# Batch 0's x and half its context loaded into rooms of their own, x's layernorm first, key stacks of the first group issued by ScalarE, and new orders

## The reference

```
h  = layernorm(x)                       # over the last axis, no weights
Q  = h @ Wq.T + bq;  K = ctx @ Wk.T + bk;  V = ctx @ Wv.T + bv
attention with 16 heads of 32, softmax over the 512 keys
x  = x + tanh(g_xattn) * (attention @ Wo.T + bo)
h  = layernorm(x)
e  = argmax(h @ router_w + router_b) of 8 experts, gate = its softmax value
x  = x + tanh(g_ffn) * gate * (h @ expert_w[e] + expert_b[e])
```

## Time and profile before

| | us |
|---|---|
| median of 3 runs | 1055.9 (1054.35 to 1056.93) |
| the profiled execution | 1057.68 |
| its span | 1056.0 |
| TensorE busy | 978.0 |
| ScalarE busy | 811.9 |
| VectorE busy | 745.6 |
| GpSimd busy | 262.0 |

### The profile page before, as it was taken

The page is one execution under the profiler, slowest core; times in us unless marked ns, Lnnn a source line. Parts: engine busy times, 40 slices in busy tenths (PEclk is TensorE's granted clock), DMA queues, the critical chain, the costliest instruction groups (busy, mean ns, idle before and its releaser), DMA issues.

```text
span 1056.0 us, 18686 instructions
## 1 busy us (share of the span) xinstructions
PE 978.0 (93%) x5208; PEld 641.8 (61%) x5208; DVE 745.6 (71%) x1653; ACT 811.9 (77%) x1913; POOL 262.0 (25%) x318
## 2 busy tenths in 40 slices
PE   3798999999999999999999999999999997698996
PEld 2564467656765676567656765676567545576775
DVE  5745655875787578757875787578757778797664
ACT  3688988898889888978898889888988988233431
POOL 6002200430042004200420042004201006454663
PEclk9799999999999999999999999999999989799999
DMA  6334223532443245324532453244325259144542
GB/s 213 97 90 114 79 64 98 143 85 69 115 137 89 69 110 140 89 60 117 136 81 70 117 137 84 68 116 137 86 69 132 62 166 378 56 135 137 163 138 75
DMA packets 70884, 119.37 MB, mean 113 GB/s; under 512 B 17854, under 2 KB 18878, under 8 KB 70656
## 3 DMA queue, kind: packets, MB, share of 16 engines
q1 hardware_dynamic: 64544, 99.49, 34.0%
q0 software_dynamic: 6240, 18.68, 5.5%
HBM read 50.42 MB, written 18.66 MB: 65 GB/s over the span
## 4 chain that ended last, share of the span: by engine, by line
PE 69%; ACT 10%; DVE 7%; issue 6%; DMA 3%; POOL 2%; SPq 2%; DVEq 1%; ACTq 0%; POOLq 0%
PE jb L489 11%; PE jb L490 10%; PE jb L491 10%; PE jb L532 10%; PE sc L512 9%; PE hb L522 9%; PE sc L673 6%; ACT jb L707 5%; ACT probs L695 3%; DVE maxima L819 1%; DVE e_lo L836 1%; PE hb L659 1%; PE jb L603 1%; SPq L452 1%; DMA q_stack<-q_lo 1%
## 5 line engine op out<-in xcount | busy, mean ns | idle before, releaser
L819 DVE TENSOR_REDUCE maxima<-jb 128x1 f32<-128x512 f32 x512 | 335.7, 686 | 112.0 <-PE jb L532 109.5
L707 ACT ACTIVATE jb<-jb,maxima 128x512 f32<-128x512 f32 x512 | 341.9, 678 | 41.4 <-DVE maxima L819 38.0
L695 ACT ACTIVATE probs<-sc 128x512 f32<-128x512 f32 x512 | 284.4, 605 | 40.7 <-PE sc L512 29.2
L532 PE MATMUL jb<-k_stack,q_stack 96*128 96x512 f32 x512 | 207.6, 434 | 24.4 <-ACT jb L707 10.1
L512 PE MATMUL sc<-q_stack,k_stack 98*128 98x512 f32 x512 | 183.9, 423 | 2.8 <-ACT probs L695 1.8
L532 PEld LDWEIGHTS jb<-k_stack,q_stack 96*128 96x128 f32 x512 | 95.9, 191 | 109.1 <-ACT jb L707 59.1
L522 PE MATMUL hb<-probs,values 128*32 128x512 f32 x1024 | 138.8, 616 | 1.0 <-ACT probs L695 0.7
L512 PEld LDWEIGHTS sc<-q_stack,k_stack 98*128 98x128 f32 x512 | 94.1, 191 | 67.9 <-ACT probs L695 36.6
L707 ACT ACTIVATION_READ_ACCUMULATOR jb<-jb,maxima 128x1 f32 x512 | 113.2, 221 | 0.0
L1104 POOL TENSOR_TENSOR stage<-stage,gbo 128x512 f32<-128x512 f32 x31 | 39.8, 1284 | 253.8 <-DMA stage<-in_x 253.8
L1096 POOL TENSOR_TENSOR row<-rt,tiny 128x2 f32<-128x2 f32 x15 | 12.7, 848 | 259.5 <-DVE rt L901 259.5
(11 more groups left out here) (228 smaller groups left out, 1740.3 us busy)
## 6 DMA issues: line engine op xcount, KB each, us to landing
k_stack<-k_hi SPq DMA_DIRECT2D x256, 64.0 KB, 2.0
q_stack<-q_hi SPq DMA_DIRECT2D x256, 64.0 KB, 2.0
stage<-in_x SPq DMA_DIRECT2D x63, 256.0 KB, 3.0
stage<-in_ctx_t SPq DMA_DIRECT2D x32, 256.0 KB, 3.2
k_stack<-k_lo SPq DMA_DIRECT2D x128, 64.0 KB, 2.0
q_stack<-q_lo SPq DMA_DIRECT2D x128, 64.0 KB, 2.0
e_lo<-in_ew SPq DMA_DIRECT2D x8, 1024.0 KB, 10.8
rows<-row SPq DMA_DIRECT2D x30, 257.5 KB, 3.4
```

Source lines behind the costliest of these rows:

```text
L532: nc.tensor.matmul(jbs[j][:], q_stack[g % 2][0:MAXROW, n * P:(n + 1) * P], k_stack[g % 2][0:MAXROW, h * S:(h + 1) * S], start=True, stop=T ...
L695: nc.scalar.activation(probs[:, kt % 2, h, :], scs[(16 * g + n) % NSC][:], ACT.Exp)\
L707: nc.scalar.activation(jbs[j][:], jbs[j][:], ACT.Exp, bias=maxima[g % 2][:, n:n + 1], accum_out=row_sums[g % 2][:, n:n + 1]).then_inc(s["m ...
L819: nc.vector.tensor_reduce(maxima[g % 2][:, n:n + 1], jbs[j][:], AX.X, ALU.max, negate=True)\
```

## The change

Six loads get rooms of their own, with a semaphore for each: context tiles 0 and 1 of batch 0, and its four x tiles. The code of SQ and SK becomes a function that SyncE and ScalarE can call. All lists are written anew, and the bank table with them. The core of it:

```diff
+FIRST = {("DC", 0, 0), ("DC", 0, 1), ("DX", 0, 0), ("DX", 0, 1), ("DX", 0, 2), ("DX", 0, 3)}
...
+        first_in = {kind: [sem(f"first_{kind}{n}") for n in range(NT)] for kind in ("DC", "DX")}
+        first_tiles = {"DC": [done_room[:, :], late_spots[:, :]],
+                       "DX": [row[:, n, 0:D] for n in range(2)] + [x2_t[:, n, :, :].rearrange("p k q -> p (k q)") for n in range(2)]}
...
+        def stack(eng, kind, g, h):
...
+            for j, src in enumerate(parts):
+                eng.dma_start(stk[g % 2][j * HD:(j + 1) * HD, h * S:(h + 1) * S].bitcast(F32),
+                              src[h * HD:(h + 1) * HD, :].bitcast(F32)).then_inc(landed[h], 16)
...
+                elif kind in ("SQ", "SK"):          # in scalar_program
+                    stack(act, kind, g, n)
...
 OPENING
 SP
-        "^DC0 ^DC1 ^DC2 LW1 LC ^DC3 ^DX0 LW0 ^DX1 ^DX2 LW2 ^DX3 ^0SK1 ^0SK0 LW3 ^0SK3 ^0SK2 ^0SQ0 ^0SQ1 ^0SQ2 ^0SQ3 ^0MD",
+        "^DC0 ^DX0 ^DX3 ^DX1 ^DX2 LC ^DC1 ^DC2 LW1 LW0 ^DC3 LW2 ^0SQ0 ^0SQ1 ^0SQ3 ^0SQ2 LW3 ^0MD",
 PE
-        "CS ^T4 ^0K ^0Kb ^0Kc ^T5 ^0Kd ^T6 ^T7 ^0Q ^0Qb ^0Qc ^0Qd ^1Q ^1Qb ^1Qc ^1Qd ^0M0 ^0M1 ^0M2 ^0M3 ^0M4 ^0M5 ^0M6 ^0M7",
-        "^0M8 ^1K ^1Kb ^0M9 ^0M10 ^0M11 ^1Kc ^1Kd ^0M12 ^0M13 ^0M14 ^V0 ^0M15 ^Vb0 ^V1 ^Vc0 ^0MT ^Vb1 ^Vc1 ^V2 ^Vd0 ^Vd1",
+        "CS ^T4 ^T5 ^T6 ^T7 ^0K ^0Kb ^0Kc ^0Kd ^0Q ^0Qb ^0Qc ^0Qd ^1Q ^1Qb ^1Qc ^1Qd ^0M0 ^0M1 ^0M2 ^0M3 ^0M4 ^0M5 ^0M6 ^0M7",
+        "^0M8 ^0M9 ^0M10 ^0M11 ^1K ^0M12 ^1Kb ^0M13 ^0M14 ^1Kc ^0M15 ^1Kd ^V2 ^Vb2 ^V1 ^0MT ^Vb1 ^Vc2 ^Vc1 ^V0 ^Vb0 ^0S0",
 ACT
-        "WT0 WT1 WT2 WT3 WT4 WT5 ^T4 ^T5 WT6 ^0K WT7 WT8 WT9 WT10 WT11 ^T6 ^T7 TH ^0Q WT12 WT13 WT14 WT15 ^0ME0 ^0ME1 ^0ME2",
-        "^0ME3 ^0ME4 ^0ME5 ^0ME6 ^1Q ^0ME7 ^0ME8 ^0ME9 ^0ME10 ^1K ^0ME11 ^0ME12 ^0ME13 ^0ME14 ^0ME15 ^0LN0 ^0MT ^V0 ^V1 ^0E0",
+        "WT0 ^T4 ^T5 TH WT1 WT2 WT3 ^T6 ^T7 WT4 WT5 WT6 WT7 ^0K ^0SK0 WT8 ^0Q WT9 WT10 ^0SK3 ^0SK2 ^0SK1 ^0ME0 ^0ME1 ^0ME2",
+        "^0ME3 ^0ME4 ^0ME5 ^0ME6 ^1Q ^0ME7 ^0ME8 ^0ME9 ^0ME10 ^0ME11 ^0ME12 ^0ME13 ^0ME14 ^0ME15 ^0LN0 WT11 ^0MT ^1K WT12",
+        "WT13 WT14 WT15 ^0E0 ^0E1 ^0E2 ^0E3 ^V0 ^0E4 ^V1 ^V2 ^1ME0 ^0E5 ^0E6 ^0E7 ^1ME1 ^1ME2 ^1ME3 ^0E8 ^0E9 ^1ME4 ^0E10",
 DVE
-        "WT0 WT1 ^LX0 WT2 CS WT3 ^LX1 ^LX2 WT4 ^LX3 ^0K WT5 WT6 ^T4 ^T5 ^T6 ^T7 WT7 WT8 WT9 TH ^0Q WT10 WT11 WT12 WT13 WT14",
+        "^LX0 ^LX1 ^LX2 ^LX3 ^T4 WT0 ^T5 ^T6 ^T7 WT1 WT2 WT3 WT4 WT5 WT6 TH ^0K WT7 WT8 ^0Q WT9 CS ^0M0 ^0M1 ^0M2 ^0M3 ^0M4",
 POOL
-        "^C0 ^C1 ^C2",
+        "^C0 ^LX0 ^LX1 ^LX2 ^LX3 ^C1 ^C2 ^C3",
 ORDER, POOL
-        "C3 ~~OP2 ~~OP3 LX0 LX1 LX2 LX3 ~OP0 ~~LR1 ~OP1 ~LR0 ^C0 ^C1 ^C2",
+        "~~LR1 ~OP0 ~OP1 ~LR0 ^C0 ^C1 ^C2 ~OP2 ^C3 ~OP3 ^LX0 ^LX1 ^LX2 ^LX3",
```

In the last body P items of one group stand side by side twice before (2P2 2P3, 3P1 3P2) and four times after (0P2 0P3, 2P0 2P1, 3P0 3P1, 3P2 3P3). Its ScalarE list and the closing lists:

```diff
 LAST, ACT
-        "... 3E7 3E8 3E9 3E10 3E11 W0 3E12 3E13 3E14 3E15 W1 3NM W6 W3 W2 W4 NE0 W5 RT0 RT1 W7"
+        "... 3E7 W1 3E8 3E9 3E10 3E11 3E12 3E13 W0 3E14 3E15 W6 3NM W2 W5 W4 W3 NE0 RT0 RT1 W7"
 CLOSING, PE
-        "~OP0 ~OPb0 ~OPc0 ~OPd0 ~OP2 ~OP1 ~OP3 ~OPb3 ..."
+        "~OP1 ~OP2 ~OP0 ~OPb0 ~OPb2 ~OPc0 ~OPd0 ~OP3 ..."
 CLOSING, DVE (both begin)
         "~OP2 ~OP3 W3 LO0 W7 LO1 LO2 ..."
 CLOSING, POOL
-        "~~LR1 ~OP0 ~OP1 GA0 GA2 GA3 GA5 ~OP2 GA4 ~OP3 GA1 W4 W5 ~LR0 GA6 ..."
+        "~OP0 ~~LR1 ~OP1 GA1 GA3 GA0 GA5 GA4 ~OP2 GA2 ~OP3 W4 W5 ~LR0 GA6 ..."
```

More of the change, by code:

```diff
@@ L34 @@
     "SP": [
-        "1SQ0 1SK0 1SK1 1SQ1 ~~RW2 ~~RW3 1SQ2 1SQ3 1SK2 1SK3 ^DC0 2SQ0 2SQ1 2SK0 2SQ3 2SK2 1MD 2SQ2 2SK1 2SK3 ^DC1 ~RW0 ^DC2",
-        "^DC3 ~RW1 3SK0 ~DR2 3SQ0 ~DR3 ^DX0 3SK1 ^DX1 2MD 3SQ1 ^DX2 3SQ2 ^DX3 3SK2 3SQ3 3SK3 DR0 3MD ^0SQ0 ^0SQ1 ^0SK0 ^0SK1",
-        "^0SQ2 ^0SK2 ^0SQ3 ^0SK3 ^0MD DR1",
+        "~~RW2 1SQ0 1SK0 1SQ1 1SK1 1SQ2 1SQ3 1SK2 ~~RW3 ^DC0 1SK3 2SQ0 2SQ1 2SQ2 2SK0 2SK3 1MD 2SQ3 ^DC1 2SK1 2SK2 ^DC2 ~RW0",
+        "~DR2 3SK0 ^DC3 3SQ0 ~DR3 3SQ1 ^DX0 3SK1 ^DX1 ~RW1 2MD 3SQ2 ^DX2 ^DX3 3SK2 3SK3 3SQ3 3MD ^0SQ0 ^0SQ1 ^0SK0 ^0SK1",
+        "^0SQ2 ^0SK2 ^0SQ3 DR0 ^0SK3 DR1 ^0MD",
     ],
     "PE": [
[10 rows of a table removed]
[10 rows of a table added]
     ],
     "ACT": [
[8 rows of a table removed]
[8 rows of a table added]
     ],
     "DVE": [
[5 rows of a table removed]
[5 rows of a table added]
     ],
     "POOL": [
-        "C3 ~~OP2 ~~OP3 LX0 LX1 LX2 LX3 ~OP0 ~~LR1 ~OP1 ~LR0 ^C0 ^C1 ^C2",
+        "~~LR1 ~OP0 ~OP1 ~LR0 ^C0 ^C1 ^C2 ~OP2 ^C3 ~OP3 ^LX0 ^LX1 ^LX2 ^LX3",
     ],
@@ L100 @@
     "SP": [
-        "1SQ1 1SK0 1SQ0 1SQ3 1SK1 ~~RW3 1SQ2 ~~RW2 ~DR2 1SK2 1SK3 ~DR3 2SQ0 2SQ1 2SK0 2SK2 2SK1 DR0 2SK3 1MD 2SQ2 2SQ3 3SK0",
-        "3SQ0 3SQ1 3SQ2 2MD 3SK1 ~RW1 ~RW0 3SQ3 3SK2 3SK3 3MD",
+        "1SK0 ~DR3 ~~RW2 1SQ0 1SK1 1SQ1 1SQ3 1SQ2 1SK3 1SK2 2SQ1 ~~RW3 2SQ0 ~DR2 2SK0 2SK1 2SK2 1MD 2SK3 2SQ2 2SQ3 DR0 3SQ0",
+        "3SK0 3SQ1 3SK1 2MD ~RW0 3SQ2 3SK2 ~RW1 3SK3 3SQ3 3MD",
     ],
     "PE": [
[6 rows of a table removed]
[6 rows of a table added]
     ],
     "ACT": [
[5 rows of a table removed]
[5 rows of a table added]
     ],
     "DVE": [
[3 rows of a table removed]
[3 rows of a table added]
     ],
     "POOL": [
-        "C3 ~~OP2 ~~OP3 LX0 LX1 LX2 LX3 ~~LR1 ~OP0 ~OP1 ~OP2 ~LR0 ~OP3",
+        "~~LR1 ~OP0 ~OP1 ~OP2 ~OP3 ~LR0",
     ],
@@ L130 @@
     "SP": [
-        "~DR2 W3 W0 ~~RW3 W1 W6 ~~RW2 ~DR1 ~DR3 W2 W4 W5 W7 EB ~RW0 ~RW1 ~RW3 ~RW2",
+        "~DR1 ~DR2 W1 ~~RW3 ~DR3 W0 W6 ~~RW2 W5 W2 W4 W3 W7 EB ~RW1 ~RW0 ~RW3 ~RW2",
     ],
     "PE": [
[3 rows of a table removed]
[3 rows of a table added]
         "TO25 Y24 TO26 Y25 TO27 Y26 TO28 Y27 TO29 Y28 TO30 Y29 TO31 Y30 TO32 Y31 TO33 Y32 TO34 Y33 TO35 Y34 TO36 Y35 TO37",
@@ L160 @@
 BANK_TABLE = [
-    "012310231031031031201203120103210320301301",
-    "3201321301203102310231023102031201230120310213023012012012012301201231301201202013213",
-    "21032021031031231201320132013213210021032023102310213201303210310310310321031032021023023020231031",
-    "03210203213213010320132013201301302230213231023120321302101320120120120132012013032031031030312012",
-    "01320301321321020130213021302102103310321312031230132103202130230230230213023021013012012010123023",
-    "02130102132132032012301230123023021102130103210312013021323012312312312301231230201203203202031231",
-    "23012023013013213203120312031231230023012021302103201230131203103103103120310312320321321323210310",
-    "31203231201201301321032103210310312231203230123021320312010321021021021032102103132130130131302102",
-    "10321310320320320321021302132132132121231012301230130123",
-    "012302012310230",
+    "012301230130130130213023023313201320321032",
+    "0321032010321023102310231023102310231023103201321302302302301230130131023230302301230",
+    "13201203210302103230123012302301230130132001320132031023123012312312312031201201023010131301302130",
+    "23102103120301203130213021301302130230231002310231032013213021321321321032102102013020232302301230",
+    "13201203210302103230123012302301230130132001320132031023123012312312312031201201023010131301302130",
+    "23102103120301203130213021301302130230231002310231032013213021321321321032102102013020232302301230",
+    "13201203210302103230123012302301230130132001320132031023123012312312312031201201023010131301302130",
+    "23102103120301203130213021301302130230231002310231032013213021321321321032102102013020232302301230",
+    "13201203210321021023123012301230212020120120132013201321",
+    "032120230123013",
 ]
@@ L238, in loads @@
             if kind in ("DC", "DX", "DR"):
-                if (kind, t, n) == ("DR", B - 1, NT - 1):
+                if (kind, t, n) == ("DR", B - 1, NT - 1) or (kind, t, n) in FIRST:
                     continue
@@ L418, in tile_of @@
         def tile_of(kind, t, n):
+            if (kind, t, n) in FIRST:
+                return first_tiles[kind][n]
             return late_stage if (kind, t, n) == ("DR", B - 1, NT - 1) else stage[load_of[kind, t, n][0]][:, :]
@@ L423, in wait_staged @@
                 wait(eng, s["late_in"], 16)
+            elif (kind, t, n) in FIRST:
+                eng.wait_ge(first_in[kind][n], 16)
             else:
@@ L426, in wait_staged @@
                 wait(eng, staged[slot], 16 * count)
+        def stack(eng, kind, g, h):
+            stk, parts, ready, landed = (q_stack, (q_hi, q_hi, q_lo), s["q_lo_done"], q_stacked) if kind == "SQ" \
+                else (k_stack, (k_hi, k_lo, k_hi), s["k_lo_done"], k_stacked)
+            wait(eng, ready, g + 1)
+            wait(eng, s["st_done"], 16 * (g - 1) + h + 1 - HG)
+            for j, src in enumerate(parts):
+                eng.dma_start(stk[g % 2][j * HD:(j + 1) * HD, h * S:(h + 1) * S].bitcast(F32),
+                              src[h * HD:(h + 1) * HD, :].bitcast(F32)).then_inc(landed[h], 16)
         def sync_program(sp):
@@ L433, in item @@
                     sp.dma_start(late_stage, x[t, n * P:(n + 1) * P, :]).then_inc(s["late_in"], 16)
+                elif (kind, t, n) in FIRST:
+                    sp.dma_start(tile_of(kind, t, n), (ctx_t if kind == "DC" else x)[t, n * P:(n + 1) * P, :])\
+                        .then_inc(first_in[kind][n], 16)
```

(8 more changed lines are left out.)

## The result

The changed kernel takes 1070.16 us (median of four runs, 1068.19 to 1075.17) against 1056.41 for the kernel before on the same chip: ratio 1.0139, 95% interval 1.0099 to 1.0178. It is 14 us slower; the forecast was 8 faster. The experiments ran on several chips. On most the kernel before takes 1055 to 1057; on the two chips of the last six runs it takes 1073.6 and 1069.5. On the first of these two the extra time lies in the expert stage for old and new lists alike (behind the last Ln 214.2 against 197.7 with the old ones, 225.3 against 207.0 with the new).

A forecast was written before the change was run, and what follows sets the result against it. TensorE was taken as the bound (busy 978.0 of 1056.0 us, 69% of the chain). 1057.7 - 4.0 (opening) - 3.8 (bodies) = 1049.9 profiled, 1048.1 median; own range 1044 to 1051.5, 8 in 10 1042 to 1058.

The forecast's parts named there:

- Opening: Start of kernel: query ready earlier, ScalarE idle recovered; first LN 5.1 us earlier, less 1.2 for V copies, gain about 4.0.
- ScalarE pays 12 x 0.61: Opening: issuing the first key stack's twelve pieces costs ScalarE 7.3 us of its own time, which was SyncE's before.
- Rival 2: DMA issues: issuing from two queues at once has a cost; size not given in this text; chance 0.12.
- Bodies: Seven middle bodies and the last: P items side by side save TensorE 0.3 us a pair; 3.8 us taken, 6.9 at most.
- Rival 3: Bodies: pairs starve ScalarE as halves of probs free later; seven bodies cost 11.9 us, time 1063.8; chance 0.16 in some size.
- The end: Last body and output projections: W1 ahead of 3E8, more cover for projections; costed at nothing, 2.2 us if cover fails.
- The forecast fails if the body moves by more than 1 us either way.: Sign on the middle body, 104.3 us before: a larger move fails the whole forecast, since seven bodies multiply it.
- The split that stays: End: VectorE's split W3 still ahead of LO0, GpSimd's W4 and W5 behind OP3, so its 11.48 us stays.

The follow-up runs named there:

- open_sk_sync: `open_new` with the first key stack's twelve pieces issued by SyncE ahead of the query pieces instead of by ScalarE; ratio 1.0037 to the kernel before.
- open_body_new: Kernel before with the new opening and new body lists, last body and closing as before: 1065.35 us, ratio 1.0060.
- open_new: Kernel before with only the new opening, all other lists as before: 1057.5 us against 1057.1, ratio 0.9998.
- open_end_new: `open_new` with the new last body and closing, bodies' lists as before: ratio 1.0116 to the kernel before.

## Why the prediction was wrong

- **Opening, forecast -5.1 at the first Ln and -4.0 behind it, measured -3.2 at the first Ln in the pair shown and -1.8 on average, there and behind the first body.** The mechanism was right, its size about twice too large. The key weights landed at 15.22, not 13.4, so the first M item came at 35.74, not 33.3. 0ME0 was at 37.00, forecast 36.3, but for another reason: not ScalarE's issues (the last ended at 35.91) but that M item held it. From 0ME0 to LN it was 14.4 instead of 16.0, a gain of 1.6 where I took 2.7. LN was at 51.43, forecast 49.6.
- **ScalarE pays 12 x 0.61.** Wrong for nine of the twelve: they ran beside its ACTIVATEs and inside a wait for the maxima. The first three did hold WT8, listed behind them, until 30.09.
- **Rival 2, given 0.12.** No run shows its term, a cost of issuing from two queues at once, beyond 0.28: the issues of the two overlap at 0.6 each, and only SyncE's first two took 1.50 instead of 1.22. With SyncE alone issuing (`open_sk_sync`) the first M item came at 39.25, 3.5 later than in the changed kernel.
- **Bodies, forecast -3.8: the step that failed, with the wrong sign.** The saving per pair was sized well (1.85 against 1.98 for two items, as in the earlier trace rows), but I gave 0.3 each to the end because TensorE held 69% of the chain. What stands between two P items is awaited by other engines: the pairs alone cost 0.53% (5.6 us), the new body lists as a whole, with what they do to the end, 6.6 to 7.9 (`open_body_new` against `open_new`). Rival 3 had the sign and not the rest: it priced the bodies at 11.9, and its 1063.8 was for the whole change, so that the pairs alone measured 1063.5 is chance. Its mechanism was wrong too: the second and third pair do little, and in the rows of the first it is 1MT and the P result that are late, not the halves of probs.
- **The end, forecast at nothing, 2.2 at worst: the largest miss, +9.3 to +11.1.** I looked at two places, W1's split and the first projections, and costed neither the order of blocks in the expert stage nor the clock. Shown: the cost belongs to the new lists of last body and closing (`open_end_new`). Where it lies in the changed kernel is read from its trace: 2.5 up to block 10, with 2.3 of idle that come of W1 ahead of 3E8; 4.4 between blocks 14 and 17, where two transposes stand without cover and the granted clock is 0.66 over ten microseconds; 2.6 spread over blocks 17 to 38. That these places cause the total is argued and not shown: no edit of them brought the ratio below 1.012.
- **"The forecast fails if the body moves by more than 1 us either way."** It moved by 0.67 in the profiles compared and by 1.0 over all of them, which is the mark itself; but the sign watched only the bodies, and the larger part lay behind the last Ln.
- **The split that stays.** It did: 10.27 on VectorE, beside GpSimd's two, which take 8.97 together; 11.48 before.
- **Two slips of reading.** Seven tiles stand ahead of the key weights now, four more than before and not five (the 3.0 MB are right). And on GpSimd OP0 and LR1 change places too, not only OP2 and C3; no run tests what that does.

## What to carry to other kernels

In an order that is in balance, what stands between two like items is there because someone waits for it: before a switch is saved, look up on the other engines' timelines who reads the items that move, and charge their lateness against the saving. A list that is written anew has to be costed to its last token, the tail above all: in that of the changed kernel an idle of 2.33 was followed by a granted clock of 0.66 over ten microseconds, one of 1.50 by 1.00 (960.3 to 970.3). That the idle brings the lower clock is not shown. And undoing one engine's list of a jointly fitted set tells little (it made this one 1 to 4% slower): move whole stages, or edit the fitted original. Last, compare a stage over several executions before its difference is believed: one stray wait in one profile hid a third of what the bodies cost.
